# The last two column quads of a graph kernel's second product, taken through rounded fp32 halves

## The reference

```python
def _lap_mul(A, x):
    d = 1.0 / jnp.sqrt(jnp.sum(A, axis=-1))
    return d[:, None] * (A @ (d[:, None] * x))
z = jax.nn.leaky_relu(_lap_mul(A, x) @ W1 + b1, negative_slope=0.1)
sq = jnp.sum(z * z, axis=-1)
d2 = jnp.maximum(sq[:, None] + sq[None, :] - 2.0 * (z @ z.T), 0.0)
S = jnp.exp(-jnp.sqrt(d2 + 1e-10) / 2.0)
S = jnp.where(ranks < 4, S, 0.0)        # ranks of -S in each row
out = _lap_mul(S + A, x) @ W2 + b2
return _layernorm(x + out)
```

## Time and profile before

| | us |
|---|---|
| median of 3 runs | 2693.22 |
| lowest, highest | 2692.01, 2697.63 |
| span of the profiled execution | 2759.5 |
| granted TensorE clock over the span | 0.969 of full |

### The profile page before, as it was taken

The page is one execution under the profiler, slowest core; times in us unless marked ns, Lnnn a source line. Parts: engine busy times, 40 slices in busy tenths (PEclk is TensorE's granted clock), DMA queues, the critical chain, the costliest instruction groups (busy, mean ns, idle before and its releaser), DMA issues.

```text
span 2759.5 us, 29107 instructions
## 1 busy us (share of the span) xinstructions
PE 2482.6 (90%) x9356; PEld 1722.4 (62%) x9356; DVE 2319.8 (84%) x1411; ACT 1606.7 (58%) x1905; POOL 1195.4 (43%) x987
## 2 busy tenths in 40 slices
PE   1367999999999998899999999999999987888978
PEld 0133444444677776578787877778787764666655
DVE  7998899977788888999999999999999773666766
ACT  0000000000477767999989899899988763555655
POOL 0000000000000000377778878788878956666760
PEclk9688999999999999999999999999999988999989
DMA  9999999995899960146555655555655688988975
GB/s 385 421 402 408 398 421 421 421 421 215 320 349 342 338 226 7 35 141 183 151 163 138 179 142 175 140 170 149 174 143 167 182 309 343 347 324 320 345 295 208
DMA packets 147949, 718.58 MB, mean 260 GB/s; under 512 B 19025, under 2 KB 26961, under 8 KB 86609
## 3 DMA queue, kind: packets, MB, share of 16 engines
q1 hardware_dynamic: 124384, 670.49, 65.6%
q0 software_dynamic: 18800, 37.77, 5.7%
q10 hardware_dynamic: 4608, 8.39, 0.8%
HBM read 680.40 MB, written 36.18 MB: 260 GB/s over the span
## 4 chain that ended last, share of the span: by engine, by line
PE 56%; issue 10%; ACT 10%; DVE 9%; DMA 7%; POOL 3%; another core or an unknown queue 3%; SPq 0%; ACTq 0%; POOLq 0%; DVEq 0%
PE PS L767 17%; PE PS L866 5%; PE PS L868 5%; PE PS L867 5%; DMA ring<-at 4%; ACT R L1141 3%; PE PS L834 3%; PE PS L910 3%; PE PS L921 3%; PE PS L911 3%; PE PS L830 2%; PE PS L831 2%; ACT ah_t L1191 2%; DVE R L1621 2%
## 5 line engine op out<-in xcount | busy, mean ns | idle before, releaser
L1299 POOL TENSOR_TENSOR al<-ring,ah 128x1024 fp32r<-128x1024 f32 x264 | 644.0, 2441 | 180.5 <-ACT ah L1112 168.7
L1621 DVE MAX8 R<-R 128x8 f32<-128x8192 f32 x64 | 555.9, 8685 | 68.1 <-ACT R L1141 67.9
L1141 ACT ACTIVATE R<-PS 128x1024 f32<-128x1024 f32 x512 | 518.1, 1018 | 114.1 <-PE PS L874 83.1
L1624 DVE FIND_INDEX8 R<-R,R 128x8 uint32<-128x8192 f32 x64 | 555.9, 8685 | 0.3 <-issue 0.3
L1272 POOL CAST zst<-zh 128x128 fp32r<-128x128 f32 (+1 forms) x64 | 26.2, 410 | 1113.2 <-DVE zl L1556 811.5
L866 PE MATMUL PS<-zh,zst 128*128 128x512 f32 x1024 | 407.3, 398 | 28.6 <-ACT PS L1127 12.7
L868 PE MATMUL PS<-zh,zst 128*128 128x512 f32 x1024 | 400.4, 391 | 0.0
L867 PE MATMUL PS<-zl,zst 128*128 128x512 f32 x1024 | 400.1, 391 | 0.0
L1456 POOL DMA_INDIRECT R<-xs_dram,R x256 | 279.7, 1093 | 145.2 <-issue 75.5
L1127 ACT ACTIVATE PS<-R 128x1024 f32<-128x1024 f32 x310 | 318.0, 1026 | 6.6
L1046 ACT ACTIVATE tiny<-rowsum 128x4 f32<-128x4 f32 x16 | 3.3, 205 | 481.2 <-DVE rowsum L1491 481.2
(11 more groups left out here) (177 smaller groups left out, 4469.9 us busy)
## 6 DMA issues: line engine op xcount, KB each, us to landing
R<-at SPq DMA_DIRECT2D x152, 1024.0 KB, 13.3
ring<-at SPq DMA_DIRECT2D x148, 1024.0 KB, 9.5
ring<-at SPq DMA_DIRECT2D x264, 512.0 KB, 3.9
cache<-at SPq DMA_DIRECT2D x117, 1024.0 KB, 20.2
raw_sq<-at SPq DMA_DIRECT2D x21, 1024.0 KB
raw_z<-at SPq DMA_DIRECT2D x20, 1024.0 KB
raw_ring<-at SPq DMA_DIRECT2D x20, 1024.0 KB
acc_dram<-R POOLq DMA_DIRECT2D x78, 256.0 KB, 5.7
```

Of the source, the lines that this page charges most:

```text
L1141: act.activation(score[j % 2][:, c * EC:(c + 1) * EC].rearrange("p (b c) -> p b c", b=2), pair(first, j, c), ACT.Copy).then_inc(copied, 1)
L1299: pool.tensor_tensor(al[:, k % SPLIT], raw[k % RAW], ah[:, k % SPLIT].bitcast(F32), ALU.subtract)\
L1621: v.max(top[:, j], score[j % 2]).then_inc(dve3, 1)
L1624: v.max_index(place[:, j], top[:, j], score[j % 2]).then_inc(placed, 1)
```

## The change

The 32 plain quads are made as the other 92 are. `plain`, `halved` and `place_of` go, all buffers alternate with u itself, and a raw buffer is always refilled after `rest_t`. The last group's x is split on chip: ScalarE rounds `xg` into `xgh_of[1]` after quad 4's rounding (`high_of_last`), VectorE subtracts it into `xgl_of[1]` ahead of quad 5's rest (`low_of_last`), and TensorE's quads with h >= 14 wait for that instead of for `xg`.

```diff
+        def high_tile(t):
+            return xsh[:, t] if t < (G - 1) * GT else xgh_of[1][:, t % GT]
         def low_tile(t):
+            if t >= (G - 1) * GT:
+                return xgl_of[1][:, t % GT]
             return xsl[:, t] if t < (G - 2) * GT else xsh[:, t + GT]
...
         def wait_halves_free(eng, u):
-            if place_of[u] >= 2:
-                eng.wait_ge(prod_t, halved[place_of[u] - 2] + 1)
+            if u >= 2:
+                eng.wait_ge(prod_t, u - 1)
...
             def load_t(u):
                 b, h = tail[u]
-                if u >= RAW_T and plain[u - RAW_T]:
-                    sp.wait_ge(prod_t, u - RAW_T + 1)
-                elif u >= RAW_T:
+                if u >= RAW_T:
                     wait_rest(sp, u - RAW_T)
...
-                if plain[u]:
-                    pe.wait_ge(xg_ok, chain_of(G - 1, False))
-                    pe.wait_ge(ld_t[u % RAW_T], 16 * (u // RAW_T + 1))
-                    for k in range(TB):
-                        i = pe.matmul(bank, xg[:, (h * TB + k) % GT], raw_t[u % RAW_T][:, k],
-                                      start=from_zero and k == 0, stop=last and k == TB - 1,
-                                      skip_group_check=True)
-                    i.then_inc(prod_t, 1)
-                    return
...
+                if h >= LAST:
+                    pe.wait_ge(xl_last_ok, 1)
+                else:
+                    pe.wait_ge(s_xs[h * TB // GT], 32)
...
+            def high_of_last():
+                act.wait_ge(s_split, 32 * (G - 1))
+                act.wait_ge(xg_ok, chain_of(G - 1, False))
+                act.activation(xgh_of[1][:, :, :], xg, ACT.Copy).then_inc(xh_last_ok, 1)
...
             for u in range(len(tail)):
-                if not plain[u]:
-                    round_t(u)
+                round_t(u)
...
+                if u == BY_POOL + 2:
+                    high_of_last()
...
+            def low_of_last():
+                v.wait_ge(xh_last_ok, 1)
+                v.tensor_tensor(xgl_of[1][:, :, :], xg, xgh_of[1][:, :, :].bitcast(F32), ALU.subtract)\
+                 .then_inc(xl_last_ok, 1)
...
+                if u == BY_POOL + 3:
+                    low_of_last()
+                rest_t(u)
```

More of the change, by code:

```diff
@@ L391, in build @@
         acc_seeded = sem("acc_seeded")
+        xh_last_ok = sem("xh_last_ok")
+        xl_last_ok = sem("xl_last_ok")
         rnd_t = sem("rnd_t")
@@ L521, in build @@
         n_heavy = [f + 1 - n_light[f] for f in range(B)]
-        plain = [h >= LAST for b, h in tail]
-        halved = [u for u in range(len(tail)) if not plain[u]]
-        place_of = {u: n for n, u in enumerate(halved)}
         def wait_rest(eng, u, part_=RESTS - 1):
-            if place_of[u] < BY_POOL:
-                eng.wait_ge(al_pool, place_of[u] + 1)
+            if u < BY_POOL:
+                eng.wait_ge(al_pool, u + 1)
             else:
-                eng.wait_ge(al_dve, RESTS * (place_of[u] - BY_POOL) + part_ + 1)
+                eng.wait_ge(al_dve, RESTS * (u - BY_POOL) + part_ + 1)
         def wait_halves_free(eng, u):
-            if place_of[u] >= 2:
-                eng.wait_ge(prod_t, halved[place_of[u] - 2] + 1)
+            if u >= 2:
+                eng.wait_ge(prod_t, u - 1)
         def wait_yf(eng, f):
@@ L966, in quad @@
                     pe.wait_ge(yf_heavy, b - HB - 1)
-                if plain[u]:
-                    pe.wait_ge(xg_ok, chain_of(G - 1, False))
-                    pe.wait_ge(ld_t[u % RAW_T], 16 * (u // RAW_T + 1))
-                    for k in range(TB):
-                        i = pe.matmul(bank, xg[:, (h * TB + k) % GT], raw_t[u % RAW_T][:, k],
-                                      start=from_zero and k == 0, stop=last and k == TB - 1,
-                                      skip_group_check=True)
-                    i.then_inc(prod_t, 1)
-                    return
-                pe.wait_ge(s_xs[h * TB // GT], 32)
-                n = place_of[u]
-                pe.wait_ge(rnd_t, n + 1)
+                if h >= LAST:
+                    pe.wait_ge(xl_last_ok, 1)
+                else:
+                    pe.wait_ge(s_xs[h * TB // GT], 32)
+                pe.wait_ge(rnd_t, u + 1)
                 for k in range(TB):
                     t = h * TB + k
-                    pe.matmul(bank, xsh[:, t], ah_t[n % 2][:, k], start=from_zero and k == 0, stop=False,
+                    pe.matmul(bank, high_tile(t), ah_t[u % 2][:, k], start=from_zero and k == 0, stop=False,
                               skip_group_check=True)
-                    pe.matmul(bank, low_tile(t), ah_t[n % 2][:, k], start=False, stop=False, skip_group_check=True)
+                    pe.matmul(bank, low_tile(t), ah_t[u % 2][:, k], start=False, stop=False, skip_group_check=True)
                 for k in range(TB):
@@ L986, in quad @@
                         wait_rest(pe, u, k * RESTS // TB)
-                    i = pe.matmul(bank, xsh[:, h * TB + k], al_t[n % 2][:, k], start=False, stop=False,
-                                  skip_group_check=True)
+                    i = pe.matmul(bank, high_tile(h * TB + k), al_t[u % 2][:, k], start=False,
+                                  stop=last and k == TB - 1, skip_group_check=True)
                 i.then_inc(prod_t, 1)
@@ L1190, in round_t @@
                 wait_halves_free(act, u)
-                act.activation(ah_t[place_of[u] % 2][:, :, :], raw_t[u % RAW_T], ACT.Copy).then_inc(rnd_t, 1)
+                act.activation(ah_t[u % 2][:, :, :], raw_t[u % RAW_T], ACT.Copy).then_inc(rnd_t, 1)
+            def high_of_last():
+                act.wait_ge(s_split, 32 * (G - 1))
+                act.wait_ge(xg_ok, chain_of(G - 1, False))
+                act.activation(xgh_of[1][:, :, :], xg, ACT.Copy).then_inc(xh_last_ok, 1)
             def load_xb(f):
@@ L1662, in rest_t @@
             def rest_t(u):
-                n = place_of[u]
-                v.wait_ge(rnd_t, n + 1)
+                v.wait_ge(rnd_t, u + 1)
                 wait_halves_free(v, u)
@@ L1667, in rest_t @@
                     ks = slice(part_ * TB // RESTS, (part_ + 1) * TB // RESTS)
-                    v.tensor_tensor(al_t[n % 2][:, ks], raw_t[u % RAW_T][:, ks], ah_t[n % 2][:, ks].bitcast(F32),
+                    v.tensor_tensor(al_t[u % 2][:, ks], raw_t[u % RAW_T][:, ks], ah_t[u % 2][:, ks].bitcast(F32),
                                     ALU.subtract).then_inc(al_dve, 1)
+            def low_of_last():
+                v.wait_ge(xh_last_ok, 1)
+                v.tensor_tensor(xgl_of[1][:, :, :], xg, xgh_of[1][:, :, :].bitcast(F32), ALU.subtract)\
+                 .then_inc(xl_last_ok, 1)
             def light_sum(b):
@@ L1726, in _ @@
                     scale_last_xg(G - 1)
-                if not plain[u]:
-                    rest_t(u)
+                if u == BY_POOL + 3:
+                    low_of_last()
+                rest_t(u)
                 for b in LIGHTS:
```

## The result

| | before | after |
|---|---|---|
| median, us | 2693.23 (5 runs) | 2714.12 (5 runs) |
| lowest, highest | 2692.01, 2697.63 | 2712.51, 2717.6 |
| span of the profiled execution | 2759.5 | 2715.8 |
| that execution's own time | not listed | 2717.6 |

The change makes the kernel slower: ratio 1.0078, 95% interval [1.0067, 1.0089], +20.9 us. The forecast was 2707, in a range of 2687 to 2727.

A forecast was written before the change was run, and what follows sets the result against it. TensorE was taken as fullest, with four resources near each other and halved quads coupling the engines; 18.1 - 3 + 0 + 0 - 1.4 = +13.7 us on 2693.2 gave 2707 us, range 2687 to 2727.

The forecast's parts named there:

- The pace of halved quads: Places 24 to 107: all-halved quads forecast at 3.62 us each, between a floor of 3.25 and 3.72 measured.
- The reason for it: All-halved quads: halves' buffers tie three engines, a rounding waits for the product two quads back; +6 to +30 us, chance 0.56.
- The pace before: Places 24 to 107 before the change: 3.405 us a quad from three dense stretches, giving +18.1 us for 84 quads.
- The long waits absorb 3 us: Places 24 to 107: 50.9 us of long waits swallow 3 us of the slowing, bounds 0 and 18.
- The opening, and the split of x: Places 6 to 23: loads set the pace, hiding TensorE's 7.1 us; split costs 0, or 2.2 us without cover.
- The end: Last two quads, 6.9 us, become 2 x 2.72 us if the halves are ready: -1.4 us.
- TensorE's 22.7 us: TensorE work saved in the last stage, 32 quads at 0.71 us each, claimed as the whole possible gain.
- DMA-bound: Rival: loads hold the pace at 3.405 us, nothing moves; 2692 us, up to +5; chance 0.19.
- TensorE-bound: Rival: TensorE was the bound and halves keep up, faster in places 24 to 107; -21.5 us, 2672; chance 0.17.
- Gathers late: Rival: more VectorE instructions slow GpSimd's gathers to a 1.2 us median; +25 us on top, 2732; chance 0.08.
- What was to show it: Signs: pace 3.5 to 3.75 us, TensorE under 90%, VectorE about 90%, `al_t` and `ah_t` waits grown, DMA share nearer 0.9.

The follow-up runs named there:

- both: Changed kernel with the variance root a quad later and roundings waiting only for the high products and rest two quads back: 2713.02 us, 1.0069.
- burst_split: Changed kernel with normalize and store three quads later (two where finishes are six apart), x-row load two later: 2702.68 us, 1.0032.
- again: Kernel before, unedited, profiled a second time: 2696.65 us.
- open_only: Kernel before with only the ten plain quads of the opening (places 6 to 23) halved, last group's x split: 2692.28 us, 0.9997.
- cost_alone: Kernel before with halves made for all 124 quads, TensorE keeping its plain products but waiting for the unused halves: 2717.93 us, 1.009.

## Why the prediction was right, and where not

- **The pace of halved quads.** Forecast 3.62 us, from a stretch of 12 quads at 3.72 and a floor of 3.25; measured 304.34 / 84 = 3.623. That it hit to the second decimal is luck: 3.62 was chosen between 3.25 and 3.72, from a sample of 12 quads whose DMA share was 0.69, where the middle has 0.97. The floor of 3.15 for work and 0.1 for gaps was near: VectorE's work is 274.8 / 84 = 3.27 a quad. The 0.35 above it are 0.305 of waiting for ScalarE and 0.05 of gaps.
- **The reason for it.** The prediction said that "the two halves' buffers tie ScalarE, VectorE and TensorE to each other", and that "ScalarE can't work such a quad ahead", the quad of 5.05 us. The runs show what is behind it: VectorE's own work, and ScalarE's quad of 5.06 us once a finish, which VectorE sits out. Taking that quad apart gave 12.3 us by the ratios (20.9 less 8.6) and 11.7 in the middle of the profiles. Not all of that is the change's: the kernel before gained 4 to 5 us by the same move. With the long quad moved in both, the halves still cost 0.5% (1.0032 against 0.9982), 13.5 us, and 14.2 us in the middle (292.65 against 278.42), with VectorE busy 94% of it. Of the buffers they show half: the tie to TensorE's product, on which the prediction rested it ("a rounding waits for the product two quads back"), is not the price, since `both` loosened it and gave 2 us at most. The depth of two between ScalarE and VectorE stayed in every run. No run has a third `ah_t`, so whether that would hide the long quad is open. The 14.0 us of waits that are left in `burst_split` were not traced further.
- **The pace before.** The term 84 x (3.62 - 3.405) = +18.1 was mis-sized on the side of before: 3.359 in `again`, which makes +22.2, 4.1 us more. The three stretches of the earlier trace rows came from the disturbed execution; they held a DMA share of 0.93 to 0.96, where the undisturbed middle has 1.01.
- **The long waits absorb 3 us.** This step failed: the waits weren't there in the other profiled execution, so the term is 0, and the sum was 3 us too low by it. That they were late loads isn't shown either: the profile calls their releaser "remote", which names none.
- **The opening, and the split of x.** Forecast 0; -0.9 in the profiles, and `open_only` at 0.9997. The loads set that pace: both openings run at a DMA share of 1.02 and 401 to 402 GB/s, and ScalarE waits for loaded blocks in both, 49.2 us in all in that of `again` and 21.6 after.
- **The end.** Forecast -1.4, measured +1.3. VectorE is busy 51.8 of 58.3 us there, where it was 42.2 of 57.0. Only half of these 9.6 us are the last two quads' rests (4 x 1.22); the others are work that it had done before place 107's product ended and now does behind it. The three terms together (22.2 - 0.9 + 1.3) are 22.6 us of stage, where the sum had 13.7. All but the opening missed in the same direction, so the point of 2707 fell 7 us short of 2714.
- **TensorE's 22.7 us.** "That is the whole gain there can be" is a bound that was never reached: 9.4 us with no halves to pay for, and 3.4 between `cost_alone` and the change (24.3 - 20.9), within the runs' spread.
- **The rivals.** DMA-bound was half right: the kernel before does wait for loads (12.0 us in the middle, 17.5 once its long quad is gone), but with the change VectorE falls behind them, and ScalarE, which waits for raw blocks before, waits for none in the middle after. TensorE-bound: it needed a pace under 3.40 with VectorE free of holes; even with more than two fifths of the holes gone it was 3.484. Gathers late: no. A gather's median in the middle is 1002 ns, where it is 947 before, far from the 1.2 us that the rival needed. It is 1077 in `burst_split`, where VectorE is busy 94% of the middle, and that kernel is the faster one. The rule of the Trainium skill that the prediction weighed ("SBUF — State Buffer", section "SBUF: two separate sides"), by which such instructions of VectorE and GpSimd shut each other out, agrees with these medians in direction; no run here shows that it is their cause. GpSimd still waits for VectorE's sums in the stage after, 9.0 us in all where it was 1.2, and ScalarE waits for no gather in the middle:

```profile
POOL R L1457 <- DVE R L1687: 9.0, 5, 3.2
```

- **What was to show it.** Right: the pace, TensorE at 90% (273.6 of 304.3) and VectorE at 90%, TensorE's waits for `ah_t` (15.3 against 8.4) and `al_t` (15.1 against 2.1) grown. Wrong: the DMA share, forecast nearer 0.9 than 0.96, is 0.97.

## What to carry to other kernels

When work moves from the fullest engine to the next one, price the second engine's sum per unit of work first: here 3.27 us of VectorE against a pace of 3.36 left little room for any wait, and the gain on TensorE, 22.7 us on paper, was 9.4 with no halves to make. An engine that is not the bound still costs its worst step if nothing lets it get ahead: spread such a step over its free quads before adding work elsewhere (here 12 us came back, where the same move gave 4 in the kernel before). And profile the kernel before twice when the profiled span lies above the median; terms taken from waits of a single execution can belong to it alone. When a tie is loosened and nothing comes, ask which part of it was left: here two buffers remained, and ScalarE, no longer waiting for TensorE's product, waited for VectorE.

## What the runs showed of the hardware

- A DMA share near 1 doesn't say that loads set the pace: after the change it is 0.97 in the middle, at 363 GB/s, with no wait of ScalarE for a loaded block, and before 1.01 at 392 GB/s, with 12.0 us of them. The rate fell by 7% and the share by 4%.
- One execution of a program on one core was 2759.5 us long in its span, with VectorE waiting up to 18.3 us for one rounding (6.8 at most in a second profiled execution, of 2694.8 us), while the seventeen other runs of it in one of the calls lay between 2688.97 and 2698.23 us.
- The gathers that GpSimd issues take longer where VectorE is fuller: a median of 947 ns with VectorE busy 83% of the middle (`again`), 1002 at 90% (after), 1077 at 94% (`burst_split`). Other engines are fuller there too, so the cause isn't isolated.
